# An attention kernel: the exponentials of two of 32 key blocks formed on VectorE

## What is computed

```python
xn = _layernorm(x)
q = _split_heads(xn @ q_w.T + q_b, h) / scale          # scale = sqrt(16)
k = _split_heads(xn @ k_w.T + k_b, h)
v = _split_heads(xn @ v_w.T + v_b, h)
scores = jnp.einsum('bhqd,bhkd->bhqk', q, k)           # 16 heads, 4096 x 4096
attn = jax.nn.softmax(scores, axis=-1)
ctx = jnp.einsum('bhqk,bhkd->bhqd', attn, v)
out = ctx @ out_w.T + out_b
...
x_fp8, x_scale = quant_fp8(xn); w_fp8, w_scale = quant_fp8(weight)
ffn = (x_fp8 @ w_fp8.T * (x_scale * w_scale) + bias).astype(bfloat16)
return x + out + ffn
```

## Time and profile before

| | |
|---|---|
| median of 3 runs | 2081.26 us (2080.5 to 2083.2) |
| the profiled execution | 2078.74 us |
| its span, first to last instruction | 2076.9 us |
| TensorE (PE) busy | 2010.5 us, 97% |
| ScalarE (ACT) busy | 1933.1 us, 93% |
| VectorE (DVE) busy | 319.0 us, 15% |
| exponentials, L559 | 1883.3 us, 2051 of 128x1024 |
| weighted sums, L1007 | 1092.2 us, 8192 instructions |
| scores, L994 | 893.0 us, 4102 instructions |
| mean granted TensorE clock | 0.993 of 2.4 GHz |

### The profile page before, as it was taken

How to read it: one execution, slowest core, us unless ns; L and a number is a source line. 1 busy time by engine, 2 the same in 40 slices (tenths; PEclk the granted TensorE clock), 3 DMA queues, 4 the chain that set the end, 5 groups by cost and what they waited for, 6 DMA issues and landing times.

```text
span 2076.9 us, 37100 instructions
## 1 busy us (share of the span) xinstructions
PE 2010.5 (97%) x13433; PEld 649.8 (31%) x13433; DVE 319.0 (15%) x798; ACT 1933.1 (93%) x2130; POOL 29.5 (1%) x53
## 2 busy tenths in 40 slices
PE   6989999999999999999999999999999999999988
PEld 4522222222222222222222222222322222222327
DVE  6631001010101001010101001010101001010106
ACT  2359999999999999999999999999999999999983
POOL 2000000000000000000000000000000000000000
PEclk9989999999999999999999999999999999999999
DMA  6960201212030201212030111212030121203022
GB/s 197 279 202 9 43 8 17 28 23 28 8 43 8 32 11 23 28 23 28 8 43 8 25 19 23 28 21 30 8 43 8 16 28 23 28 12 39 8 39 81
DMA packets 65523, 82.08 MB, mean 40 GB/s; under 512 B 9952, under 2 KB 47360, under 8 KB 62208
## 3 DMA queue, kind: packets, MB, share of 16 engines
q1 hardware_dynamic: 65472, 81.58, 19.4%
HBM read 54.79 MB, written 26.21 MB: 39 GB/s over the span
## 4 chain that ended last, share of the span: by engine, by line
PE 93%; DMA 2%; DVE 1%; issue 1%; ACT 1%; SPq 1%; ACTq 0%; DVEq 0%
PE banks L1007 49%; PE banks L994 38%; PE banks L912 2%; PE banks L1106 1%; PE banks L955 1%; ACT probs L559 1%; PE banks L923 1%; DMA k_parts<-probs 1%; DVE o_sb L776 1%; PE banks L975 0%; PE banks L1090 0%; PE banks L1097 0%; PE banks L896 0%; DMA q_st<-q_parts 0%; DMA x_all<-in_L_attn_query_dram 0%
## 5 line engine op out<-in xcount | busy, mean ns | idle before, releaser
L559 ACT ACTIVATE probs<-banks 128x1024 f32<-128x1024 f32 x2051 | 1883.3, 1372 | 8.7 <-DMA k_parts<-probs 4.7
L1007 PE MATMUL banks<-probs,v_st 128*32 128x512 f32 x8192 | 1092.2, 605 | 5.4 <-DVE o_sb L776 5.4
L994 PE MATMUL banks<-q_st,k_st 50*128 50x512 f32 x4102 | 893.0, 484 | 19.8 <-ACT probs L559 17.3
L994 PEld LDWEIGHTS banks<-q_st,k_st 50*128 50x128 f32 x4102 | 368.3, 183 | 1034.5 <-ACT probs L559 1015.5
L1007 PEld LDWEIGHTS banks<-probs,v_st 128*32 128x32 f32 x8192 | 161.6, 108 | 282.5 <-issue 261.8
L751 DVE TENSOR_REDUCE mcol<-banks 128x8 f32<-128x512 f32 x66 | 45.6, 691 | 1000.4 <-PE banks L955 1000.4
L776 DVE STREAM_TRANSPOSE o_sb<-banks 128x512 f32<-128x512 f32 x32 | 22.9, 717 | 480.0 <-PE banks L1007 480.0
L767 DVE CAST neg_row<-banks 32x128 fp32r<-32x128 f32 x33 | 9.2, 278 | 187.3 <-PE banks L975 187.3
L489 POOL COPY v_st<-v_all 128x256 f32 x32 | 12.9, 406 | 1759.4 <-PE banks L1007 1759.4
L519 ACT ACTIVATE parts<-banks,qk_bias 128x512 fp32r<-128x512 f32 x14 | 9.6, 687 | 28.6 <-PE banks L912 27.4
L519 ACT ACTIVATE probs<-banks,qk_bias 128x512 fp32r<-128x512 f32 x18 | 12.0, 686 | 26.0 <-PE banks L912 12.0
(11 more groups left out here) (80 smaller groups left out, 362.5 us busy)
## 6 DMA issues: line engine op xcount, KB each, us to landing
k_st<-k_parts SPq DMA_DIRECT2D x204, 128.0 KB, 4.3
q_st<-q_parts SPq DMA_DIRECT2D x204, 64.0 KB, 4.9
q_parts<-probs SPq DMA_DIRECT2D x9, 512.0 KB, 6.1
k_parts<-probs SPq DMA_DIRECT2D x9, 512.0 KB, 6.4
xnT_copy<-probs SPq DMA_DIRECT2D x8, 512.0 KB, 4.4
probs<-xnT_copy SPq DMA_DIRECT2D x8, 512.0 KB, 6.3
w_f<-xnT_copy SPq DMA_DIRECT2D x16, 256.0 KB, 5.3
out_dram<-qt SPq DMA_DIRECT2D x16, 256.0 KB, 2.1
```

The source lines that it names most:

```text
L559: act.activation(probs[:, at:at + wide * CHUNK].rearrange("p (t c) -> p t c", t=wide), banks[:, bank:bank + wide, :], ACT.Exp, scale=SCALE ...
L994: last = pe.matmul(banks[:, WIDE * (e % BUFS) + r - r0, :], k_mm[rows, kt * P:(kt + 1) * P], blocks[rows, qb // GROUPS], start=True, stop= ...
L1007: last = pe.matmul(banks[VCOLS * qb:VCOLS * (qb + 1), 6, :], v_st[:, kt, :], probs[:, at:at + CHUNK], start=(kt == 0), stop=(kt == KT - 1) ...
```

## The change

In every unit the key blocks 15 and 31 (`D_ROWS`) are no longer given to ScalarE. Their eight score tiles go one at a time into `misc` (`d_scores`), in the loops `D_SLOTS`: 5, 6, 9, 16 for the first block and 18, 25, 27, 34 for the second. VectorE forms the exponentials from them (`d_exponentials`), half a block (two tiles, 1024 columns) at a time: w_q and the bias of q are scaled by 0.25 log2(e) 2^23, so a score plus a constant, converted to int32, is the bit pattern of a power of two with a linear mantissa; exponent and mantissa are masked apart into `powers` and `bits`, and a polynomial in the mantissa times the power of two gives the result in `d_probs`. TensorE adds the two blocks to the sums in the even loops 26 and 44 (`D_SUM`). ScalarE's exponentials use the scale 1/UNIT, and are 60 to a unit, 120 to a head. The maxima jobs stand in loops 42 and 44 of both units, their turn in loop 47.

`d_probs` takes the place of w_q, w_k, w_v and the bias of v once they have been used; `powers` and `bits` that of the parts buffers 2 and 3, so VectorE waits, ahead of its first use, for their last save. `exp_of` and `banks_user` become simpler, since 120 divides by three.

```diff
+LOG2E = 1.4426950408889634
+ONE_BITS = 0x3F800000
+MANTISSA_BITS = 0x007FFFFF
+EXP_BIAS = 1013270912.0
+POLY = (-0.1511656492948532, 12.309608459472656, 23.089841842651367, 37.712982177734375)
...
+    D_ROWS = (KT // 2 - 1, KT - 1)
+    A_ROWS = [kt for kt in range(KT) if kt not in D_ROWS]
+    D_SLOTS = ((5, 6, 9, 16), (18, 25, 27, 34))
+    D_SUM = (26, 44)
+    HALF = 2 * CHUNK
+    MAX_FIRST, MAX_TURN = 42, 47
+    UT4 = QB * len(A_ROWS)
+    UE = UT4 // WIDE
...
+    UNIT = LOG2E * 2.0 ** 23
...
@@ ScalarE @@
             root(0)
+            act.wait_ge(w_in["q"], 16)
+            act.activation(w_sb["q"][:, :, :], w_sb["q"][:, :, :], ACT.Copy, scale=SCALE * UNIT).then_inc(q_scaled, 1)
             copy_turned(0, 0, SAVED_0)
             act.wait_ge(bias_in, 16 * 8)
+            act.activation(qk_bias[:, 0, :], qk_bias[:, 0, :], ACT.Copy, scale=SCALE * UNIT).then_inc(q_scaled, 1)
...
@@ VectorE @@
+                def d_exponentials(h, u, d, half, job):
+
+                    done = (u * len(D_ROWS) + d) * 2 + half
+                    steps = h * (UNITS * len(D_ROWS) * 2 * D_STEPS) + done * D_STEPS
+                    words, tops = bits.bitcast(I32), powers.bitcast(I32)
+                    result = d_probs[:, half * HALF:(half + 1) * HALF]
+                    if d or half:
+                        dve.wait_ge(c.d_ready, h * (UNITS * len(D_ROWS) * 2) + done)
+                    for i in range(2):
+                        dve.wait_ge(c.misc_full, job + (i + 1))
+                        dve.tensor_scalar(words[:, i * CHUNK:(i + 1) * CHUNK], misc, -EXP_BIAS, EXP_BIAS,
+                                          ALU.max, ALU.add).then_inc(c.misc_free, 1)
+                    dve.wait_ge(c.misc_free, job + 2)
+                    dve.tensor_scalar(tops[:, :], words[:, :], EXPONENT_BITS, None, ALU.bitwise_and
+                                      ).then_inc(c.d_chain, 1)
+                    dve.wait_ge(c.d_chain, steps + 1)
+                    dve.tensor_scalar(words[:, :], words[:, :], MANTISSA_BITS, ONE_BITS, ALU.bitwise_and,
+                                      ALU.bitwise_or).then_inc(c.d_chain, 1)
+                    dve.wait_ge(c.d_chain, steps + 2)
+                    if d and not half:
+                        dve.wait_ge(c.pv_done, h * STEPS + (PV_0 + u * KT + SUM_OF_D[d - 1] + 1))
+                    dve.scalar_tensor_tensor(out=result, in0=bits[:, :], scalar=POLY[0], in1=bits[:, :],
+                                             op0=ALU.add, op1=ALU.mult).then_inc(c.d_chain, 1)
+                    for j in (1, 2):
+                        dve.wait_ge(c.d_chain, steps + (2 + j))
+                        dve.scalar_tensor_tensor(out=result, in0=result, scalar=POLY[j], in1=bits[:, :],
+                                                 op0=ALU.add, op1=ALU.mult).then_inc(c.d_chain, 1)
+                    dve.wait_ge(c.d_chain, steps + D_STEPS)
+                    dve.scalar_tensor_tensor(out=result, in0=result, scalar=POLY[3], in1=powers[:, :],
+                                             op0=ALU.add, op1=ALU.mult).then_inc(c.d_ready, 1)
...
+                    for i in (2, 3):
+                        dve.wait_ge(parts_saved[i], saved_in_half_1(i, len(range(i // 2, NCH, 3))))
                     quantise_weight()
...
@@ TensorE @@
+                def d_scores(h, u, d, qb, job):
+
+                    pe.wait_ge(c.misc_free, job)
+                    if u == 0 and qb == 0:
+                        pe.wait_ge(c.k_in[D_ROWS[d] // (KT // 2)], h * LOADS + LOADS)
+                    score_tile(misc, D_ROWS[d], u, qb).then_inc(c.misc_full, 1)
```

More of the change, by code:

```diff
@@ L111, in program @@
         out_scale = sb("out_scale", [P, 1])
-        parts = {i: sb(f"parts{i}", [P, PARTS, CHUNK]) for i in (2, 3)}
+        powers = sb("powers", [P, HALF])
+        bits = sb("bits", [P, HALF])
+        PART_WORDS = PARTS * CHUNK
+        parts = {2 + i: t.rearrange("p (a c) -> p a c", a=PARTS) for i, t in enumerate((powers, bits))}
         q_st = sb("q_st", [P, S // GROUPS])
@@ L241, in exp_of @@
         def exp_of(tile):
-            u, r = divmod(tile, UT4)
-            return u * UE + r // WIDE, r % WIDE, min(WIDE, UT4 - r // WIDE * WIDE)
-        def banks_user(e):
-            return BUFS if e >= BUFS else e + HE - ((HE - 1 - e) // BUFS * BUFS + e)
-        def ring_user(tile):
-            u, r = divmod(tile, UT4)
-            r -= RING
-            if r < 0:
-                u, r = u - 1, r + RING
-                r += (UT4 - 1 - r) // RING * RING
-            return u * KT + r // QB
+            return tile // WIDE
+        SUM_ORDER = []
+        for e in range(UE):
+            SUM_ORDER += [(e, i, None, kt) for i, kt in enumerate(A_ROWS) if exp_of(QB * i + QB - 1) == e]
+            if e in D_SUM:
+                SUM_ORDER.append((e, None, D_SUM.index(e), D_ROWS[D_SUM.index(e)]))
+        SUM_OF_A = {i: pos for pos, (_, i, _, _) in enumerate(SUM_ORDER) if i is not None}
+        SUM_OF_D = {d: pos for pos, (_, _, d, _) in enumerate(SUM_ORDER) if d is not None}
+        def ring_user(tile):
+            before, t = divmod(tile - RING, HT)
+            u, r = divmod(t, UT4)
+            return before * STEPS + u * KT + SUM_OF_A[r // QB]
         tok = "(t p) d -> p t d"
@@ L718, in _ @@
             QUANT_STEPS = 6
+            D_STEPS = 5
             qn = [0]
@@ L758, in negate @@
                 def negate(link0):
-                    above = 0.0 if c.full else HEADROOM / SCALE
+                    above = 0.0 if c.full else HEADROOM * UNIT
                     chain(dve.tensor_scalar(neg_full[:, :], mcol[:, :], -1.0, -above, ALU.mult, ALU.add), link0 + 1)
@@ L822, in attend @@
                     neg_count[0] = h * 2 + 2
-                    maxima(job, lk)
+                    for d in range(len(D_ROWS)):
+                        for half in range(2):
+                            d_exponentials(h, 0, d, half, job + (QB * d + 2 * half))
+                    maxima(job + QB * len(D_ROWS), lk)
                     take_sums(h, 0, lk + MAX_LINKS)
                     normalise(h, 0, lk + (MAX_LINKS + SUM_LINKS - 2))
+                    job = job + c.unit_jobs
+                    for d in range(len(D_ROWS)):
+                        for half in range(2):
+                            d_exponentials(h, 1, d, half, job + (QB * d + 2 * half))
                     if not c.full:
@@ L841, in attend @@
                     lk = lk + (MAX_LINKS + SUM_LINKS)
-                    maxima(job + (c.max_jobs + 1), lk)
+                    maxima(job + QB * len(D_ROWS), lk)
                     take_sums(h, 1, lk + MAX_LINKS)
@@ L883, in _ @@
             pe.wait_ge(consts, 9)
-            for n in "qkv":
+            for n in "kv":
                 pe.wait_ge(w_in[n], 16)
@@ L991, in scores @@
                             pe.wait_ge(c.k_in[r // (UT4 // 2)], h * LOADS + LOADS * (1 + nxt))
-                        g = qb % GROUPS
-                        rows = slice(g * GROUP, g * GROUP + STACK)
-                        last = pe.matmul(banks[:, WIDE * (e % BUFS) + r - r0, :], k_mm[rows, kt * P:(kt + 1) * P],
-                                         blocks[rows, qb // GROUPS], start=True, stop=True)
+                        last = score_tile(banks[:, WIDE * (e % BUFS) + r - r0, :], A_ROWS[i], u, qb)
@@ L996, in scores, with score_tile @@
                     last.then_inc(c.st_done, 1)
-                def weighted_sum(h, t):
-                    u, kt = divmod(t, KT)
-                    if kt == 0:
+                def score_tile(out, kt, u, qb):
+                    blocks = q_mm[:, u * UG:(u + 1) * UG].rearrange("k (c j x) -> k j c x", j=QB // GROUPS, x=P)
+                    rows = slice(qb % GROUPS * GROUP, qb % GROUPS * GROUP + STACK)
+                    return pe.matmul(out, k_mm[rows, kt * P:(kt + 1) * P], blocks[rows, qb // GROUPS],
+                                     start=True, stop=True)
```

98 lines of the change are left out of this document (58 added, 40 removed).

## The result

The changed kernel takes **2134.87 us** (median of 4 runs, 2131.91 to 2136.35), the kernel before 2081.49 us (4 runs, 2080.5 to 2083.2): ratio 1.0253, 95% interval 1.024 to 1.0266. The direction was forecast, not the size: +53 us where I had +18.6, and the case that came true in size is my second rival (the clock), at the place where I had put it. The profiled execution took 2133.51 us, its span is 2131.7 us.

What follows compares the result with a forecast made beforehand. ScalarE was taken to bound the kernel, TensorE to pace the changed one: 113.0 + 2 x 0.85 + 3.4 + 0.7 = 118.8 us per head against 117.7, x 16 = +18, plus 1 outside: 2100 us, range 2056 to 2150.

Steps and rivals of the forecast that it cites:

- second rival: TensorE's new idle time in the heads drops its clock to half: 2112 to 2150 us, chance 0.20.
- sum per head: TensorE's work 113.0 plus waits 2 x 0.85, 3.4 and 0.7: 118.8 us per head against 117.7.
- the maxima's wait: In unit 1 TensorE's second maxima job waits 3.4 us because VectorE quantises x before reading the first maximum.
- Outside the heads: Scaling w_q and the bias, VectorE's wait for the last saves, and row loads: 1 us added.
- TensorE becomes the pacemaker: TensorE's work per unit, 56.5 us, exceeds ScalarE's 55.0, so it sets 113.0 us per head.
- my own sign of being wrong: The forecast is wrong if, among other signs, exponentials still follow each other at 0.917 us.
- VectorE's durations: VectorE's chain per half block: copy 0.69, mask 0.69, fused step 1.22 us.
- single tile: Each of eight lone score tiles per unit costs TensorE 0.33 us, as a pair does: 2.6 us.
- first rival: Single tiles cost less than 0.33 us; from 0.23 the heads take 117.7. Case 2055 to 2087 us, chance 0.21.
- 0.35 us per unit in which TensorE waits for ScalarE: In loops without extra work TensorE can catch up only some 0.7 us per head, 0.35 per unit.
- bank's wait: TensorE waits 0.85 us before tile 6 until VectorE has copied tile 5 out of the one bank.
- rival 3: VectorE is in time, the quantising or the chain fitting: 113.7 us per head, 2017 us, chance 0.06.

Runs made afterwards that it cites:

- e5_sum_at_48: Changed kernel with VectorE quantising x after the maxima, plus the second VectorE block's sum in loop 48 instead of 44: 2050.09 us.
- e8_fill_with_few: Changed kernel, TensorE's wait for the maxima's reading kept but filled with two long fp32 matmuls: 2114.04 us, ratio 1.0152.
- e10_narrow_tile: e7_spread with each single tile's score matmul 128 columns wide instead of 512: 2012.67 us.
- e7_spread: Changed kernel, x quantised after the maxima; tiles 6 to 8 in loops 26, 30, 36, sums 28, 48, maxima 42, 45, turn 49: 2024.28 us.
- e6_tile_at_26: Changed kernel with x quantised after the maxima, plus tiles 6 and 7 in loops 26 and 28 instead of 25 and 27: 2025.62 us.

## Why the prediction was right or wrong

**The step that failed** is the sum per head, "113.0, + 2 x 0.85, + 3.4, + 0.7", in which TensorE's clock has no term; the runs showed 2.1 us per head in its place, 34 us in all. I had put it into the second rival, at 0.20, with "dense work on both sides" against it. All 16 waits were followed by a fall, though the work on both sides was dense. The rival's size for one fall, 3 us, was right for the eight long ones (2.9) and twice too much for the eight short ones (1.5), hence 34 us where it had 48 for a fall in each head. The row I had was the right one: 2.3 us of idle time ahead of a half-clock window. (The 4.2 us of that row I misread: they end at 133.20, inside the window from 129, and not ahead of it.) A forecast wait longer than 2.3 us should have had the clock in the sum.

| per head, us | forecast | measured |
|---|---|---|
| first unit | 56.5 + 0.85 + 0.35 = 57.7 | 57.88 |
| the maxima's wait | 3.4 | 2.93 |
| clock | none | 34 / 16 = 2.1 |
| a head, less the 117.7 of before | +1.1 | +3.14 |

Times 16 the last line is +50, where I had +18. Outside the heads I had +1, and it is +4.5: the first exponential starts at 135.3 instead of 132.1, and from the last one to the end it is 1.3 us more. The first part isn't a cost of the change alone: in experiments with the same code there it starts between 131.1 (e5_sum_at_48) and 136.1 (e8_fill_with_few), and I don't know why.

Point by point:
- *TensorE becomes the pacemaker*: wrong, and this is the second step that failed. The idle time is about what I had said (154.4 / 16 = 9.7 us per head for scores, against 8 to 9), but my own sign of being wrong came true: exponentials still follow each other at ScalarE's pace, 55 of the 60 in a unit, and the loss sits in five dry spots. "57.7" for a unit was near the measured 57.88 by luck, see below.
- *VectorE's durations* (0.69, 0.69, 1.22): right to 0.01 us. Costs per column from neighbours of the same source and kind held.
- *The single tile, 0.33*: it is 0.23 or 0.24. In TensorE's timeline a group of two pairs takes 0.66 to the next sum, with a single tile 0.90:

```profile
688.40 0.73 PE L1063 MATMUL banks<-q_st,k_st 50*128 50x512 f32 x4
...
689.06 1.06 PE L1089 MATMUL banks<-probs,v_st 128*32 128x512 f32 x8
...
695.44 0.96 PE L1063 MATMUL banks<-q_st,k_st 50*128 50x512 f32 x5
...
696.34 1.06 PE L1089 MATMUL banks<-probs,v_st 128*32 128x512 f32 x8
```

  The Trainium skill's page "TensorE: Matmul & The Clock Gate", section "Back-to-back issue gap", gives N/2.4 + 2.5 ns for an isolated warm matmul, by my estimate 0.22 us for 512 columns. The trace, with 0.23 to 0.24, is on its side, not on mine. My first rival, which rested on it, was still wrong: it said that the heads take 117.7 from 0.23 us on. The 0.8 us per unit that I had too much here I had too little elsewhere, next point.
- *0.35 us per unit in which TensorE waits for ScalarE*: too small. With tiles at 0.24 TensorE's own unit is, by an estimate from my sum, some 55.8, with the bank's wait 56.7, and 57.88 was measured: some 1.2 us per unit in which it waits for ScalarE (no row counts them apart). Two errors of 0.8 us hid each other in "57.7". I read the unit now so: with three pairs of banks TensorE can't get far ahead of ScalarE, single tiles that stand alone vanish in its slack, and what exceeds the lead (a sum, the maxima jobs, the bank's wait) makes ScalarE dry. The timelines above and e10_narrow_tile show this; how much of it placing alone can win stays open, since e5_sum_at_48 and e7_spread won next to nothing.
- *The bank's wait, 0.85*: right, once a unit: 0.91 by the loads, 0.59 by the matmuls, and 0.8 us per unit went with it in e6_tile_at_26.
- *The maxima's wait, 3.4*: place and kind right, 0.5 us too long. The quantising took its 4.0 us; VectorE's last step ended 0.3 us after the first job was issued (719.84 against 719.54), where I had 0.75.
- *VectorE in time* (rival 3) was wrong for this kernel. It came true in e6_tile_at_26, where neither the quantising nor the bank is waited for: 2025.62 us, where I had said 2017.
